# Scores of two heads on two halves of TensorE's rows, and the causal mask for the maxima split between VectorE and TensorE

## The chip, the cores and the metric

One core of a Trainium2 chip runs the whole program. The metric is the device time of one execution in microseconds, lower is better; the median of several runs is given. TensorE multiplies (weights are loaded beside it), VectorE, ScalarE and GpSimd compute element by element, SyncE issues transfers. Banks are the eight accumulation buffers that TensorE writes, 128 partitions of 512 fp32 each.

## What is computed

```python
x = x + 0.5 * ffn(layernorm(x))      # 8 experts, each token goes to the one with the largest gate
x = x + attn(layernorm(x))
x = x + 0.5 * ffn(layernorm(x))

def attn(x):                          # 8 sequences of 256 tokens, 128 wide, 16 heads of 8
    xn = x * rsqrt(mean(x * x) + 1e-6) * norm_w
    q, k, v = heads(xn @ Wq.T + bq), heads(xn @ Wk.T + bk), heads(xn @ Wv.T + bv)
    scores = where(causal, -inf, q @ k.T / sqrt(8))
    return xn + merge(softmax(scores) @ v) @ Wo.T + bo
```

## The kernel before

The program has three parts: a first expert layer, the attention, a second expert layer. Each expert layer first routes (gate logits, a chain of small VectorE operations in `route_pick`, `route_prob` and `route_slot`, then `dispatch` on GpSimd, which scatters 16 tiles of tokens with one indirect DMA each), then works through 23 tiles of tokens sorted by expert. The change touches only the attention and what runs beside it.

**Numbers and scores.** fp32 q and k are split into three bf16 parts, whose products are stacked along the partitions: 6 blocks of 8 rows are the 48 rows of one head (`JROWS`). `qz` holds q, `ks` holds k, two buffers of each for alternate sequences. Before, a pair of heads (j = 0 and 1) lies on 96 rows, and `qz` has zeros where the other head of the pair stands, so that one product over 96 rows gives one head's scores. Scores are computed twice. `scores_q` gives them with queries on the partitions, plus the causal mask, which TensorE adds as a product of the identity with a table; `max_unit` on VectorE takes each query's maximum from it. GpSimd splits the maxima into three bf16 parts (`max_split`), TensorE transposes them (`turn_max`), ScalarE copies them (`max_copy`), and SyncE's queue carries them as three more rows into `qz` (`max_rows`, 99 rows then). `scores_k` gives the scores with keys on the partitions and the maximum already subtracted; `exp_unit` on ScalarE takes exp into `pT`; `mask` on GpSimd sets what is above the diagonal to zero; `pv` on TensorE multiplies with v, four heads on four column groups of 32.

**Order.** A step is one sequence, in two halves of eight heads (four pairs); a half has six units, U0 to U5, each one bank of 512 columns. Step b computes `scores_k` of sequence b and, unit by unit beside it, `scores_q` of sequence b + 1. Before, U0, U1, U3 and U4 are early units, each one pair with keys 0 to 127 and all queries (for `scores_q` queries 128 to 255 and all keys); U2 and U5 are late units, two pairs with the other 128 keys (for `scores_q` queries and keys 0 to 127). `scores_q` uses banks 0 and 1, `scores_k` banks 2 and 3. Each engine's order is written out by hand; semaphores count units (`a_s` scores_q done, `a_mx` maxima, `a_st` scores_k done, `a_e` exps, `a_pm` masks, `a_pv` pv calls). `pv` of the half's first pairs (pp = 0) is issued behind U4 and waits for two masks, that of the others behind U1 of the next half and waits for all four. Between the units stand the products of the sequence before: `out_copy` on ScalarE, `turn_out` (transposes, one per 128 queries, banks 7 and 6), `normalise` on VectorE, `turn_norm`, a copy on ScalarE, `project`, `add_out` on VectorE. GpSimd also does the `residual` operations, 0.7 us each, between masks. Steps 1 to 4 stand in a loop of two iterations, the others are written out. SyncE's queue carries splits to DRAM (`split_stores`), loads them again as stacks (`stack_load`, four transfers per half) and `max_rows`, strictly one behind the other. `late_routing` places gate products of the second expert layer inside step 7, and `last_mask`, `late_stats` and the routing chain run on VectorE at its end; `ln_scale` on GpSimd stands between its masks and its scatters.

## Time and profile before

| | |
|---|---|
| median of 3 runs | 318.89 us (318.65 to 320.3) |
| profiled execution | 317.4 us, its span 315.3 us |
| TensorE busy | 271.4 us, 86% of the span, 2368 products |
| VectorE busy | 212.2 us, 67% |
| GpSimd busy | 185.7 us, 59% |
| ScalarE busy | 149.2 us, 47% |
| mean granted TensorE clock | 0.961 |

The span goes from the first to the last instruction of the profiled execution; the rest of its time lies around it. Busy shares are means over three parts with different limits: the attention steps lie between about 124 and 237 us of the span, the two expert layers on either side. Products overlap in TensorE and their ends are modelled, so start-to-start times are what a product costs in a row of them.

### The profile page before, as it was taken

The numbers are of one execution on the slowest core, as the hardware profiler recorded it, in microseconds if no ns is written. First come the engines' busy times: TensorE is split into PE (matmuls) and PEld (weight loads), VectorE is DVE, ScalarE is ACT, GpSimd is POOL, SyncE is SP. The second block draws the span as 40 slices with busy tenths as digits, with TensorE's granted clock in tenths as the row PEclk, the third lists the DMA queues.
The fourth block names the chain that finished last, engine by engine and source line by source line (L and its number), as shares of the span: only waits on it lengthen the run. The fifth ranks groups of instructions, "written<-read, shape, count | busy, mean of one in ns | idle before, by whom it ended". The sixth has DMA issues, their size and how long they took to land.

```text
span 315.3 us, 7921 instructions
## 1 busy us (share of the span) xinstructions
PE 271.4 (86%) x2368; PEld 219.5 (70%) x2368; DVE 212.2 (67%) x685; ACT 149.2 (47%) x362; POOL 185.7 (59%) x332
## 2 busy tenths in 40 slices
PE   7724999999997778999989999998977759999980
PEld 6724999999994544656656565665646658999970
DVE  4956058888539568986657777776587744888860
ACT  2300076666206613676656667666541007666620
POOL 7587815445726313786767787888647740555561
PEclk9999999999999996999999999999976799999997
DMA  6974232221041733552433522110001143122100
GB/s 184 397 313 122 60 80 55 68 67 32 17 133 41 202 109 112 165 166 87 135 95 115 157 74 70 58 55 2 5 10 45 56 113 91 49 68 67 30 21 0
DMA packets 34388, 29.37 MB, mean 93 GB/s; under 512 B 4109, under 2 KB 28818, under 8 KB 34353
## 3 DMA queue, kind: packets, MB, share of 16 engines
q1 hardware_dynamic: 29696, 23.52, 25.1%
q0 software_dynamic: 2496, 4.27, 4.3%
q10 hardware_dynamic: 2160, 1.14, 1.4%
q8 instruction: 18, 0.29, 0.4%
q14 instruction: 18, 0.14, 0.1%
HBM read 17.08 MB, written 12.55 MB: 94 GB/s over the span
## 4 chain that ended last, share of the span: by engine, by line
PE 48%; POOL 16%; issue 9%; DMA 9%; DVE 9%; SPq 4%; ACT 2%; POOLq 1%; ACTq 0%; DVEq 0%
PE bank L1291 12%; PE bank L1302 11%; POOL disp_d L479 7%; PE bank L1448 4%; PE bank L1420 3%; PE bank L1396 3%; POOL pT L574 2%; PE bank L1426 2%; DMA row<-in_x 2%; PE bank L1393 2%; SPq L406 2%; POOL row L470 2%; PE bank L1283 2%; PE bank L1401 2%; DMA disp_d<-row,slot 2%
## 5 line engine op out<-in xcount | busy, mean ns | idle before, releaser
L746 ACT ACTIVATE pT<-bank 128x512 f32<-128x512 f32 x96 | 56.5, 600 | 43.0 <-PE bank L1426 29.2
L1056 DVE TENSOR_REDUCE mh<-bank 128x2 f32<-128x512 f32 x64 | 42.1, 683 | 10.1 <-PE bank L1396 9.9
L1302 PE MATMUL bank<-experts,hT 128*128 x368 | 48.9, 276 | 0.0
L1291 PE MATMUL bank<-xsT,ew 128*128 128x128 f32 x368 | 48.8, 276 | 0.1
L1222 PE MATMUL bank<-zero 128*128 128x128 f32 x268 | 37.3, 305 | 10.5 <-DVE rowi L934 4.7
L574 POOL TENSOR_SCALAR_AFFINE_SELECT pT<-pT 128x512 f32<-128x512 f32 x62 | 40.2, 651 | 9.4 <-ACT pT L746 9.3
L1302 PEld LDWEIGHTS bank<-experts,hT 128*128 128x128 f32 x368 | 44.8, 192 | 0.5 <-issue 0.3
L1291 PEld LDWEIGHTS bank<-xsT,ew 128*128 128x128 f32 x368 | 44.7, 192 | 0.5 <-issue 0.2
L1222 PEld LDWEIGHTS bank<-zero 128*128 128x128 f32 x268 | 35.8, 219 | 11.0 <-DVE rowi L934 4.7
L664 ACT ACTIVATE hT<-bank,ew 128x128 f32<-128x128 f32 x92 | 28.9, 365 | 28.7 <-PE bank L1291 28.7
L941 DVE TENSOR_SCALAR hT<-bank,ew 128x128 f32<-128x128 f32 x92 | 28.0, 346 | 21.3 <-PE bank L1291 19.9
L479 POOL DMA_INDIRECT disp_d<-row,slot x32 | 32.3, 1009 | 13.3 <-issue 13.3
L487 POOL DMA_INDIRECT out<-ys_sb,xs_sb x23 | 22.6, 983 | 29.2 <-DVE ys_sb L965 27.7
L487 POOL DMA_INDIRECT x_d<-ys_sb,xs_sb x23 | 22.8, 991 | 24.1 <-DVE ys_sb L965 22.8
L652 ACT ACTIVATE xq<-xs_sb 128x128 f32<-128x128 f32 x46 | 22.5, 492 | 28.8 <-DMA xs_sb<-disp_d 28.8
L1060 DVE TENSOR_REDUCE mh<-bank 128x4 f32<-128x512 f32 x32 | 22.1, 690 | 19.3 <-PE bank L1405 19.3
L1420 PE MATMUL bank<-qz,ks 99*128 99x512 bf16 x64 | 24.8, 390 | 1.9 <-DMA qz<-mT 1.7
L1396 PE MATMUL bank<-ks,qz 96*128 96x256 bf16 x128 | 25.4, 281 | 0.0
L949 DVE TENSOR_SCALAR ew<-experts 128x644 f32 x46 | 22.4, 494 | 2.4 <-issue 1.8
L1448 PE MATMUL bank<-pT,va 128*32 128x256 f32 x256 | 20.9, 398 | 1.8 <-DVE pT L1182 1.5
L957 DVE TENSOR_TENSOR yb<-bank,ew 128x128 f32<-128x128 f32 x46 | 13.4, 292 | 12.8 <-PE bank L1302 10.0
L1393 PE MATMUL bank<-cb 128*128 128x256 bf16 x64 | 18.1, 283 | 1.6 <-DMA ks<-sp_d 1.3
(140 smaller groups left out, 465.9 us busy)
## 6 DMA issues: line engine op xcount, KB each, us to landing
sp_d<-spl SPq DMA_DIRECT2D x32, 192.0 KB, 2.5
experts<-in_experts SPq DMA_DIRECT2D x8, 578.0 KB, 9.5
qz<-sp_d SPq DMA_DIRECT2D x32, 96.0 KB
ks<-sp_d SPq DMA_DIRECT2D x32, 96.0 KB
xs_sb<-disp_d SPq DMA_DIRECT2D x46, 66.0 KB, 1.9
row<-in_x SPq DMA_DIRECT2D x4, 256.0 KB, 5.2
row<-x_d SPq DMA_DIRECT2D x4, 256.0 KB, 3.6
disp_d<-pad ACTq DMA_DIRECT2D x12, 66.0 KB
```

The source lines that it names most:

```text
L479: pool.indirect_dma_start(disp_d[f][:, :], bass.IndirectOffsetOnAxis(ap=slot[:, t:t + 1], axis=0), row[:, t, :], None).then_inc(d_tok[f], 16)
L487: pool.indirect_dma_start(target[:, :], bass.IndirectOffsetOnAxis(ap=xs_sb[:, t % RING, ID:ID + 1].bitcast(U32), axis=0), ys_sb[:, t % OUT ...
L574: pool.affine_select(out=p_, in_=p_, pattern=[[0, 4], [1, P]], compare_op=ALU.is_ge, fill=0.0, base=0, channel_multiplier=-1).then_inc(a_p ...
L664: mm = act.activation(hT[:, par, c, :], bank[2 + 2 * par][:, c * P:(c + 1) * P], ACT.Relu, bias=ew[:, k, HID + c:HID + c + 1])
L746: act.activation(pT[:, u, :], bank[2 + u % 2][:, :], ACT.Exp, scale=SCALE).then_inc(a_e, 1)
L1056: dve.tensor_reduce(mh[:, half, 1, :, 2 * pp + w], bank[u % 2][:, :].rearrange("p (h n) -> p h n", h=2), AX.X, ALU.max).then_inc(a_mx, 1)
L1222: pe.matmul(bank[b][:, 0:P], zero[:, :], zero[:, :], start=True, stop=True)
L1291: mm = pe.matmul(bank[2 + 2 * (k % 2) + c // 2][:, (c % 2) * P:(c % 2 + 1) * P], ew[:, k % WRING, c * P:(c + 1) * P], xsT[:, k % 2, :], st ...
L1302: mm = pe.matmul(bank[6 + k % 2][:, 0:D], hT[:, k % 2, c, :], w2.rearrange("p a c -> p (a c)"), start=(c == 0), stop=(c == HC - 1))
L1396: mm = pe.matmul(ov[:, j, :], qz[k][0:SROWS, half, j, pair - 4 * half, P:T], ks[k][0:SROWS, pair, :], start=False, stop=True, **MM_BANK)
L1420: mm = pe.matmul(ov, ks[k][0:KROWS, pair, 0:P], qz[k][0:KROWS, half, :, pair - 4 * half, :], start=True, stop=True, **MM_BANK)
L1448: mm = pe.matmul(o[32 * h:32 * h + 32, pp * T:(pp + 1) * T], va[:, k, 0, 8 * j + pair, :], pT[:, 3 * pp + h // 2, j * T:(j + 1) * T], star ...
```

## The change

- Heads of even and odd j no longer share rows with zeros: j = 0 lies on partitions 0 to 47 (and its three maxima rows on 48 to 50), j = 1 on 64 to 111 (and 112 to 114). The fill of `qz` goes. `max_rows` is two transfers.
- Units hold one j each: U0, U1 and U4, U5 are early (two pairs, one j), U2 and U3 late (all four pairs, one j). In a unit the `scores_k` product of a head of one j and the `scores_q` product of a head of the other j are issued in turn.
- `scores_q` has three banks (0, 1, 6). Its mask comes from TensorE in late units and for sequence 0; elsewhere `tensor_tensor_reduce` on VectorE adds `msk` and takes the maximum, 256 keys of one head at a time, writing the sum back to the bank.
- `turn_max`, both `turn_out`, `turn_norm` and `project` share bank 7, so they wait for each other. `project` and `add_out` move one half later, `turn_out` of the second query tile into the second half, `pv` of the first pairs behind U5 with three masks awaited.
- The loops over steps 1 to 4 are written out, and the `turn` instructions that stood before the masks in them go.

```diff
-SROWS = 2 * JROWS
-MROW = SROWS
-KROWS = MROW + 3
+KROWS = JROWS + 3
+JBASE = P // 2
...
+LOWEST = -3e38
+QB = (0, 1, 6)
...
+        def unit(u):
+
+            late = u in (2, 3)
+            return late, 0 if late else 2 * (u // 4), 4 if late else 2
...
-                    rows_j = slice(JROWS * j, JROWS * (j + 1))
-                    for t, buf in ((0, qz[k][rows_j, half, j, :, :]),
+                    rows_j = slice(JBASE * j, JBASE * j + JROWS)
+                    for t, buf in ((0, qz[k][rows_j, half, :, :]),
...
-                sp.dma_start(qz[k][MROW:MROW + 3, half, :, :, :].rearrange("s j i n -> s (j i n)"), mT[:, half, :]
-                             ).then_inc(a_m[half], 16)
+                for j in range(2):
+                    sp.dma_start(qz[k][JBASE * j + JROWS:JBASE * j + KROWS, half, :, :].rearrange("s i n -> s (i n)"),
+                                 mT[12 * j:12 * j + 12, half, :]).then_inc(a_m[half], 16)
...
-                pool.memset(qz[k][:, :, :, :, :].rearrange("p h j i n -> p (h j i n)").bitcast(F32), 0.0
-                            ).then_inc(static_s, 1)
...
+            def mask(b, half, n):
+
+                pool.wait_ge(a_e, 12 * b + 6 * half + (2, 3, 4, 6)[n])
                 need(pool, a_pm, 8 * b + 4 * half + n - 3)
-                if not isinstance(b, int):
-                    pool.tensor_tensor(turn[:, n:n + 1], zero[:, 0:1], zero[:, 0:1], ALU.add)
-                if late:
-                    p_ = pT[:, 3 * pp + 2, :].rearrange("p (h n) -> p h n", h=4)
+                if n in (1, 2):
+                    p_ = pT[:, n + 1, :].rearrange("p (h n) -> p h n", h=4)
                 else:
-                    p_ = pT[:, 3 * pp:3 * pp + 2, :].rearrange("p u (j n) -> p (u j) n", j=2)[:, :, 0:P]
+                    p_ = pT[:, n // 3 * 4:n // 3 * 4 + 2, :].rearrange("p u (i n) -> p (u i) n", i=2)[:, :, 0:P]
                 pool.affine_select(out=p_, in_=p_, pattern=[[0, 4], [1, P]], compare_op=ALU.is_ge, fill=0.0,
                                    base=0, channel_multiplier=-1).then_inc(a_pm, 1)
...
-            with pool.Fori(0, 2) as i:
-                for k in range(2):
-                    for half in range(2):
-                        step(2 * i + 1 + k, half)
-            for b in (5, 6, 7):
+            for b in range(1, B):
...
-                need(act, a_pv, 2 * (2 * b + half - 1) + 1 + u // 3
-                     if not isinstance(b, int) or 2 * b + half > 0 else 0)
+                need(act, a_pv, 2 * (2 * b + half - 1) + (1 if u < 2 else 2)
+                     if 2 * b + half > 0 else 0)
...
-                    if u == 3 and half == 1 and not first:
+                    if u == 4 and half == 1 and not first:
...
-                pp, w = divmod(u, 3)
+                late, p0, heads = unit(u)
                 if u == 0:
                     need(dve, a_mb, 2 * b + half - 1)
-                if w < 2:
-                    dve.tensor_reduce(mh[:, half, 1, :, 2 * pp + w],
-                                      bank[u % 2][:, :].rearrange("p (h n) -> p h n", h=2), AX.X, ALU.max
-                                      ).then_inc(a_mx, 1)
+                top = mh[:, half, 0 if late else 1, 1 - u % 2, p0:p0 + heads]
+                if b == 0 or late:
+                    i1 = dve.tensor_reduce(top, bank[QB[u % 3]][:, :].rearrange("p (h n) -> p h n", h=heads),
+                                           AX.X, ALU.max)
                 else:
-                    dve.tensor_reduce(mh[:, half, 0, :, 2 * pp:2 * pp + 2].rearrange("p j i -> p i j"),
-                                      bank[u % 2][:, :].rearrange("p (h n) -> p h n", h=4), AX.X, ALU.max
-                                      ).then_inc(a_mx, 1)
+                    n = 512 // heads
+                    for m in range(heads):
+                        sc = bank[QB[u % 3]][:, m * n:(m + 1) * n]
+                        i1 = dve.tensor_tensor_reduce(sc, sc, msk[:, T - n:T], 1.0, LOWEST, ALU.add, ALU.max,
+                                                      top[:, m:m + 1])
+                i1.then_inc(a_mx, 1)
...
-                o = bank[7 - qt][:, :].rearrange("p (g j c) -> p g j c", g=NPAIR, j=2)
+                o = bank[7][:, :].rearrange("p (g j c) -> p g j c", g=NPAIR, j=2)
...
+                    if b >= 2 and (half, u) == (0, 0):
+                        add_out(b - 2)
                     if not first:
-                        if half == 0 and u == 5:
+                        if half == 0 and u == 4:
                             normalise(b - 1, 0)
                         if half == 1 and u == 0:
                             normalise(b - 1, 1)
-                        if half == 1 and u == 5:
-                            add_out(b - 1)
...
+            dve.memset(msk[:, 0:P], 0.0).then_inc(msk_s, 1)
+            dve.tensor_copy(msk[:, P:T], cst[:, C_MS:C_MS + P]).then_inc(msk_s, 1)
             for u in range(6):
                 max_unit(0, 0, u)
+            quad_vbias(3)
+            dve.wait_ge(msk_s, 2)
...
+            add_out(5)
...
+                dve.wait_ge(a_e, 12 * (B - 1) + 6 + (2, 3, 4, 6)[n])
...
+            def head(k, half, p_, j, top):
+
+                return (qz[k][JBASE * j:JBASE * j + top, half, p_, :],
+                        ks[k][JBASE * j:JBASE * j + top, 4 * half + p_, :])
+
+            def scores_q_waits(b, half, u):
+
                 if u == 0:
...
+                    pe.wait_ge(a_stk[b % 2][half], 64 * (b // 2 + 1))
+                need(pe, a_mx, 12 * b + 6 * half + u - 2)
+
+            def scores_q_part(b, half, u, m, masked=False):
+
+                late, p0, heads = unit(u)
+                n = 512 // heads
+                q_, k_ = head(b % 2, half, p0 + m, 1 - u % 2, JROWS)
+                return pe.matmul(bank[QB[u % 3]][:, m * n:(m + 1) * n], q_[:, 0:P] if late else q_[:, P:T], k_[:, 0:n],
+                                 start=not masked, stop=True, **(MM_BANK if masked else {}))
+
+            def scores_k_part(k, half, u, m):
+
+                late, p0, heads = unit(u)
+                n = 512 // heads
+                q_, k_ = head(k, half, p0 + m, u % 2, KROWS)
+                return pe.matmul(bank[2 + u % 2][:, m * n:(m + 1) * n], k_[:, P:T] if late else k_[:, 0:P],
+                                 q_[:, T - n:T], start=True, stop=True)
+
+            def scores_q_mask(u):
+
+                heads = unit(u)[2]
+                pe.matmul(bank[QB[u % 3]][:, :].rearrange("p (h n) -> p h n", h=heads)[:, :, 512 // heads - P:],
+                          ident_b, maskS.unsqueeze(1).broadcast_to((P, heads, P)), start=True, stop=False, **MM_BANK)
+
+            def scores_first(half, u):
+
+                scores_q_waits(0, half, u)
+                scores_q_mask(u)
+                for m in range(unit(u)[2]):
+                    mm = scores_q_part(0, half, u, m, masked=True)
                 mm.then_inc(a_s, 1)
 
...
+            def scores(b, k, half, u, more):
+
                 if u == 0:
...
+                    pe.wait_ge(a_m[half], 32 * (b + 1))
                 need(pe, a_e, 12 * b + 6 * half + u - 1)
...
+                if more:
+                    scores_q_waits(b + 1, half, u)
+                    if unit(u)[0]:
+                        scores_q_mask(u)
+                for m in range(unit(u)[2]):
+                    mk = scores_k_part(k, half, u, m)
+                    if more:
+                        mq = scores_q_part(b + 1, half, u, m, masked=unit(u)[0])
+                mk.then_inc(a_st, 1)
+                if more:
+                    mq.then_inc(a_s, 1)
...
-                pe.wait_ge(a_pm, 8 * b + 4 * half + 2 * pp + 2)
+                pe.wait_ge(a_pm, 8 * b + 4 * half + pp + 3)
...
+            def step(b, half, more, first=False):
+
+                k = b % 2
                 for u in range(6):
...
+                    scores(b, k, half, u, more)
                     if u == 1 and half:
                         pv(b, k, 0, 1)
                     elif u == 1 and not first:
                         pv(b - 1, 1 - k, 1, 1)
...
+                    if (half, u) == (0, 0) and b >= 2:
+                        project(b - 2)
+                    if (half, u) == (0, 2):
+                        pe.wait_ge(a_mtc, 2 * b + 1)
+                        need(pe, a_x, b - 1)
+                        turn_max(b, 1)
+                    if (half, u) == (0, 3) and first:
                         pe.wait_ge(q_r, NU)
...
+                    if (half, u) == (0, 4) and not first:
+                        pe.wait_ge(a_mtc, 2 * b + 2)
+                        turn_out(b - 1, 0)
+                    if (half, u) == (0, 5) and first:
+                        pe.wait_ge(a_mtc, 2)
                         quad_v(4)
...
+                    if u == 5:
                         pv(b, k, half, 0)
...
+                    if (half, u) == (1, 0) and not first:
+                        pe.wait_ge(a_an, 2 * b - 1)
+                        turn_out(b - 1, 1)
+                    if (half, u) == (1, 2) and more:
+                        if first:
+                            pe.wait_ge(q_vc, NU)
+                        need(pe, a_an, 2 * b)
+                        pe.wait_ge(a_mtc, 2 * b + 2)
+                        turn_max(b + 1, 0)
+                    if (half, u) == (1, 4) and not first:
+                        if more:
+                            pe.wait_ge(a_mtc, 2 * b + 3)
+                        turn_norm(b - 1)
                     if not more:
                         late_routing(half, u)
...
+            for b in range(1, B):
                 for half in range(2):
...
+                    step(b, half, b < B - 1)
+            project(6)
...
+            pe.wait_ge(a_an, 2 * B - 1)
             turn_out(7, 1)
```

## Rows read from the trace of the kernel before

**Rows 1.** Busy time of each engine (and instructions), TensorE clock, DMA share, GB/s, one step.

```profile
164.90:178.30 13.40, 13.31 (x145) 8.50 (x143) 9.46 (x18) 8.68 (x17) 10.37 (x30) 1.00 0.41 120
```

**Rows 2.** Timeline of TensorE, step 4: start, us, engine, line, operation, [idle before].

```profile
177.69 0.71 PE L1478 MATMUL bank<-wt,anT 128*128 128x128 f32 x4
178.23 0.39 PE L1426 MATMUL bank<-qz,ks 99*128 99x256 bf16 x2
178.46 0.38 PE L1401 MATMUL bank<-cb 128*128 128x512 bf16 x1
178.68 0.39 PE L1405 MATMUL bank<-ks,qz 96*128 96x128 bf16 x4
178.90 0.38 PE L1420 MATMUL bank<-qz,ks 99*128 99x512 bf16 x1
...
185.72 0.38 PE L1420 MATMUL bank<-qz,ks 99*128 99x512 bf16 x1
...
186.60 0.38 PE L1396 MATMUL bank<-ks,qz 96*128 96x256 bf16 x2
186.91 0.64 PE L1448 MATMUL bank<-pT,va 128*32 128x256 f32 x8
...
187.70 0.39 PE L1426 MATMUL bank<-qz,ks 99*128 99x256 bf16 x2
```

**Rows 3.** Timeline of TensorE in step 7.

```profile
219.33 0.80 PE L1420 MATMUL bank<-qz,ks 99*128 99x512 bf16 x2
...
230.96 0.44 PE L1472 MATMUL bank<-ident_t,an 128*128 128x128 f32 x2 [0.64 <-DVE an L1100]
...
231.48 1.06 PE L1252 MATMUL bank<-wgc,gT 128*128 128x8 f32 x8
```

**Rows 4.** Timeline of GpSimd behind step 7.

```profile
238.06 0.19 POOL L468 TENSOR_SCALAR vs<-mv 128x2 f32<-128x2 f32 x1 [0.54 <-DVE mv L1169]
...
255.61 1.22 POOL L479 DMA_INDIRECT disp_d<-row,slot  x1 [0.30 <-issue]
```

**Rows 5.** Groups by line and shape: busy us, mean ns | idle before, releaser.

```profile
L1056 DVE TENSOR_REDUCE mh<-bank 128x2 f32<-128x512 f32 x64 | 42.1, 683 | 10.1 <-PE bank L1396 9.9
...
L1448 PE MATMUL bank<-pT,va 128*32 128x256 f32 x256 | 20.9, 398 | 1.8 <-DVE pT L1182 1.5 <-POOL pT L574 0.3
...
L569 POOL TENSOR_TENSOR turn<-zero 128x1 f32<-128x1 f32 x32 | 6.2, 195 | 11.5 <-ACT pT L746 11.5
...
L1107 DVE TENSOR_TENSOR row<-bank,row 128x256 f32<-128x256 f32 x4 | 1.7, 420 | 0.4 <-PE bank L1478 0.4
```

**Rows 6.** Timeline of ScalarE, steps 3 and 6.

```profile
178.66 0.60 ACT L746 ACTIVATE pT<-bank 128x512 f32<-128x512 f32 x1 [0.60 <-PE bank L1426]
...
208.79 0.36 ACT L753 COPY mT<-bank 24x256 bf16<-24x256 bf16 x1
209.11 0.60 ACT L746 ACTIVATE pT<-bank 128x512 f32<-128x512 f32 x1
209.61 0.58 ACT L759 COPY oT<-bank 128x512 f32<-128x512 f32 x1
```

**Rows 7.** Timeline of GpSimd, step 6.

```profile
211.52 0.64 POOL L574 TENSOR_SCALAR_AFFINE_SELECT pT<-pT 128x512 f32<-128x512 f32 x1
212.13 0.72 POOL L521 TENSOR_TENSOR res<-res,rows 128x256 f32<-128x256 f32 x1
212.81 0.64 POOL L574 TENSOR_SCALAR_AFFINE_SELECT pT<-pT 128x512 f32<-128x512 f32 x1
```

**Rows 8.** Timeline of SyncE's DMA queue, steps 3 and 4.

```profile
176.88 0.37 SPq L392 DMA_DIRECT2D sp_d<-spl  x1
...
181.30 0.70 SPq L406 DMA_DIRECT2D ks<-sp_d  x1
182.54 0.77 SPq L411 DMA_DIRECT2D qz<-mT  x1
```

**Rows 9.** Timeline of TensorE, step 2.

```profile
159.10 0.39 PE L1420 MATMUL bank<-qz,ks 99*128 99x512 bf16 x1 [1.69 <-DMA qz<-mT]
```

176 lines of the change are left out of this document (43 added, 133 removed).

## The prediction

> **What bounds the kernel now.** I read the page's first part (the table above), then the busy time of each engine step by step, then single engines' timelines inside a step. A step is one sequence (256 tokens) of the attention loop, two halves of eight heads with six units each: U0 to U5, a bank of scores per unit for `scores_k` and one for `scores_q`. TensorE is the busiest engine of the span, but that is a mean over stages. In a steady step the reader is to see TensorE busy 13.31 of 13.40 us, VectorE 9.46, ScalarE 8.68, GpSimd 10.37 [rows 1]: TensorE paces the steps. Step 4 starts at 178.90, its second half at 185.72 [rows 2], step 7 at 219.33 [rows 3]: steps 4 to 6 take 13.48 us each. Behind step 7 the bound changes: GpSimd waits 0.54 us for statistics of sequence 6 at 238.06 and then issues scatters one after another to 255.61, with 0.30 us of issue between [rows 4]. What comes late at 238.06 comes late at the end.
>
> **The change, part by part.** *Products.* An early unit (256 keys) had one `scores_k` product of 512 columns, a mask product of 256 and two `scores_q` products of 256. Columns are what costs: 512 take 0.22 us from start to start (178.46 to 178.68), four times 128 the same (178.68 to 178.90) [rows 2]. So a half streamed 8192 columns, 3.5 us. Now `scores_k` has 3072, `scores_q` 3072 and the mask 1024 (late units only). Heads of even j lie on partitions 0 to 50, of odd j from 64 on, and each k product is followed by a q product on the other half of the array's rows, into another bank. If a pair runs in the time of one, a half streams 4096 columns: 1.76 us, 1.7 less. The trace has no row tiles. Its nearest row is `pv` on four column groups: 256 products of 398 ns are busy 20.9 us together [rows 5], some five at a time. That bounds a pair between the time of one (0.11 us for 256 columns) and of two; I take one, since that row too is an array cut into parts.
>
> *Switches.* `pv` gives a price on the other side. The two score products before it start at 186.60 and have streamed by 186.82; `pv` starts at 186.91, 0.09 later [rows 2]. I take 0.10 us for each switch between whole and cut array; the lower bound is nothing, if 64-row products are no switch, the upper 0.2, twice the row. A half had four switches and gets eleven: around the transposes or projections behind U0 and U4, around the mask products of U2 and U3, around two `pv`. The Trainium skill (TensorEngine Tiling (Array Packing), Key Properties) says that a change of tiling mode drains the engine, and that tiles run independently. The trace agrees for the 128x32 tiles, 0.09 us; no run here shows 64-row tiles. By that rule all eleven are paid.
>
> *The chain inside a half* is then what counts, for TensorE's own sum is only 6.8 less 1.7 plus 0.7, 5.8 us. `pv` of the first pairs now stands behind U5 and needs three masks, not two, since both late units hold heads of all pairs. From U0: U0 0.22, four products of `project` 0.54 (177.69 to 178.23), U1 0.22, the `pv` of the half before 0.79 (186.91 to 187.70), U2's mask 0.22 [rows 2], then 0.49 to its exp (the last of four pairs starts 0.165 in, and the exp began 0.32 behind the second product that follows 178.23 [rows 2, 6]), and four switches: 2.88. From there the exp 0.60 [rows 6], on GpSimd a mask 0.61, a residual operation 0.68, the next mask 0.64 [rows 7], hand-overs twice 0.07 (ScalarE's start shows 0.04), then `pv` 0.79 and the next half's U0: 3.46. Together 6.34 us. In a first half ScalarE makes it longer: from U2's exp (2.88) 0.50 to `max_copy`, 0.32 to U3's exp, 0.50 to `out_copy`, its 0.58 [rows 6], 0.1, `turn_out` (0.54 as `project`), two switches, U5 0.22, `pv` 0.79: 6.6. A step is 12.95 us instead of 13.48. Score products lose 3.4 us a step; 0.5 arrive.
>
> *VectorE.* Eight reductions of 512 per step, 683 ns each, become sixteen `tensor_tensor_reduce` of 256 with a mask from SBUF. The trace has none. Nearest is the addition of 256 from a bank, 420 ns; the other end is 683 each, if the write-back and the read-out cost as much as half the elements [rows 5]. I take 420, the same two operands and elements: VectorE's step goes from 9.46 to 10.7, below 12.95, so it is hidden by the chain; at 683 it is 14.9. The Trainium skill (VectorE: DVE Perf Modes, Two Vector instructions with no wait between them) counts an operation that also reads out an accumulator as two instructions; no run here shows it, and it lies between these ends. The third bank lets TensorE run one unit further ahead of the maxima. TensorE idles 0.09 us a step [rows 1], so that gains nothing.
>
> *The maxima's rows.* `max_rows` becomes two transfers on SyncE's queue, 0.77 us of issue each. Queued behind the second are stores and loads, from 176.88 to 182.00 in a half with a store, and behind those the next `max_rows`, at 182.54 [rows 8]; U0 of the next half waits for its rows. The queue's round in such a step is 1.6 + 5.12 + landing + 3.74 from U0 to the end of `max_copy` (2.88 + 0.50 + 0.36). Landing took at most 3.18 (U0 at 185.72 didn't wait [rows 2, 8]) and at least its issue, 0.77; I take 2.5, between them and nearer to the upper, since loads go in front. That gives 13.0, as long as the chain; 3.18 gives 13.6. Once TensorE has waited 1.69 for these rows [rows 9]; I keep that wait. Step 0, with stores in both halves, gains nothing for that reason.
>
> *Hidden edits.* The `turn` instructions (6.2 us in all [rows 5]), the loops and the fill of `qz` go from GpSimd, which waits for exps and tiles there; without that cover a `turn` was 0.2 us. `msk` is built while VectorE waits for the first loads. `quad_vbias`(3) moved ahead of `quad_rest` costs up to 0.68 there, as a reduction of 512; the third bank saves TensorE about as much in the same place.
>
> *The end of the attention.* `project`(5) moves into step 7, and `pv` of its first half waits for the third mask, which stands behind `ln_scale` on GpSimd. The second gate's logits follow that `pv`, so `route_pick` and `normalise`(6,0) on VectorE are a `pv` late, 0.8 us. And `turn_out`(6,1) shares bank 7 now: TensorE waits for `normalise`(6,0) right behind U0 of the second half. Before, it waited at 230.96 for both, with U1, U2, `pv`, ranks and the third gate's transposes already issued, and that gate's logits followed at 231.48 [rows 3]. Now all of these come after the wait: `turn_out` 0.54, U1 0.22, `pv` 0.79, ranks and transposes (put at 0.54, as four products), 0.49 to U2's exp, 0.50, the gate's copy 0.58 as `out_copy`, switches 0.4: 4.06 us from `normalise`(6,0) to these logits. I put `normalise`(6,0) half a microsecond ahead of the old wait, so it was 1.0; 3.0 later. Then `pv`, whose mask now stands behind `route_pick`, and `project`(6) come before `add_out`(6), 1.33 us, less 0.3 for the last exp, which no longer ends last: 1.0. The sum, 4.8 us, meets the statistics awaited at 238.06. Bounds: 0 if the wait is covered, 6 if TensorE's clock falls in it.
>
> **Sum.** Steps 1 to 6: six by 0.5, 2.9 less. The end: 4.8 more. 315.3 and 2.1 around the span are 317.4 profiled; 319.3. The median shown, 318.89, lies 1.5 above its profile: 320.8, say 321.0.
>
> **Rivals.** (a) *Switches cost nothing*: 12 halves by 0.4, and 0.8 at the end, 5.6 less: 315.4, faster. For it: the array is cut by rows, not by columns as in `pv`. Against: the 0.09. It decides below 0.03 us a switch. (b) *The end is covered*: `normalise`(6,0) is done before TensorE needs it: 316.2, faster. Against it: TensorE did wait for it at 230.96. (c) *The pairs don't overlap*, so the change doesn't do what it says: U0, U1 and U2 0.22 longer each, 0.66 by 12 halves: 328.9. For it: no row here shows row tiles. (d) *SyncE's queue*: the wait of 1.69 in each of steps 1 to 4: 327.8. For it: the wait happened once. Against: 185.72 didn't wait. (e) *VectorE becomes the bound*, 14.9 a step: six by 1.95, 332.7. For it: two reads and a write on one bank.
>
> **Chances.** Forecast 0.48, with a range of its own of 318.5 to 323.5; (a) 0.15, (b) 0.10, (c) 0.12, (d) 0.10, (e) 0.05. A change within 0.5% (317.3 to 320.5) is about what a measurement can't tell from none. Faster takes (a), (b) and an edge of the forecast, 0.26; same the forecast's lower part, 0.21; slower the rest, 0.53. The range reaches from (a) to (c): 315 to 329.
>
> **What would show it.** Right: products on the two halves of the array that start almost together; gaps of 0.1 us at each switch; steps near 13 us with TensorE clearly idle, ended by GpSimd's mask in front of `pv`; sixteen reductions near 0.42 us; TensorE waiting some 3 us for `normalise` in step 7. Wrong: steps below 12.3; steps above 13.6 with VectorE full, or with the rows' transfer as releaser; score products one behind the other; scatters that start behind step 7 as early as now.

## The result: 334.6 us, and the profile after

| | before | after |
|---|---|---|
| median of 4 executions | 318.77 us | 334.63 us |
| profiled execution, its span | 317.4, 315.3 us | 333.28, 331.2 us |
| mean granted clock of TensorE | 0.961 | 0.924 |
| TensorE busy in the span | | 267.2 us (81%) |

The change makes the kernel slower, 1.0415 times (95% interval 1.0315 to 1.0515). Ratios, here and below, count undisturbed executions alone, medians count all. The forecast was 321.0, with a range to 329. The direction was right; of 15.9 us between the two profiled executions it had foreseen 1.9.

First the stretches of the profile after, cut at U0 of each step (step 0 to step 7, the last one cut at 240.09); the columns are the stretch, its length, busy time and instructions of TensorE, its weight loads, VectorE, ScalarE and GpSimd, the granted clock (1.00 is 2.4 GHz, 0.50 is 1.2 GHz), DMA share, GB/s.

```profile
124.29:140.11 15.82, 12.95 (x129) 6.29 (x130) 13.49 (x42) 8.70 (x16) 11.00 (x22) 0.68 0.57 168
140.11:153.66 13.55, 10.32 (x151) 5.22 (x148) 10.48 (x43) 8.47 (x17) 9.07 (x21) 1.00 0.36 105
153.66:170.42 16.76, 13.71 (x151) 6.50 (x152) 10.81 (x42) 8.52 (x17) 8.94 (x21) 0.80 0.34 97
170.42:184.41 13.99, 11.06 (x150) 5.62 (x151) 10.57 (x42) 8.65 (x18) 9.71 (x22) 1.00 0.40 117
184.41:198.54 14.13, 11.06 (x150) 5.65 (x150) 10.57 (x42) 8.58 (x17) 9.27 (x22) 1.00 0.37 110
198.54:214.18 15.64, 12.54 (x150) 6.08 (x150) 12.18 (x51) 8.58 (x17) 10.43 (x24) 0.89 0.17 54
214.18:228.20 14.02, 11.07 (x151) 5.64 (x151) 12.06 (x51) 8.59 (x17) 11.62 (x26) 1.00 0.10 33
228.20:240.09 11.89, 8.45 (x84) 5.65 (x85) 6.29 (x25) 5.04 (x10) 5.80 (x13) 1.00 0.01 2
240.09:260.30 20.21, 14.84 (x104) 8.99 (x105) 9.44 (x46) 5.63 (x13) 9.11 (x11) 0.58 0.07 21
```

The same of before, steps 0, 2 and 5 (step 2 holds the wait of [rows 9] at full clock):

```profile
123.58:137.05 13.47, 13.08 (x122) 8.01 (x121) 11.93 (x19) 8.95 (x16) 9.58 (x21) 0.88 0.61 176
...
150.46:165.54 15.08, 13.37 (x145) 8.44 (x143) 9.55 (x18) 8.71 (x18) 10.39 (x30) 1.00 0.41 115
...
192.28:205.53 13.25, 13.22 (x146) 8.37 (x144) 10.39 (x27) 8.81 (x18) 10.64 (x25) 1.00 0.21 62
```

Three things stand in these lines. TensorE's own work fell from 13.3 to 11.06 us a step, as it should. The steps didn't: those at full clock take 13.6 to 14.1 us, some 3 us of it TensorE's idle time. And steps 0, 2, 5 and the end have a clock below 1.00 and are the long ones. The kernel before has low clock too, in its step 0 (0.88) and behind step 7: over the 20.21 us that begin 11.89 us behind U0 of step 7, the last stretch above, it has 0.70 where the changed kernel has 0.58.

```profile
231.22:251.43 20.21, 15.53 (x104) 12.40 (x103) 14.94 (x81) 4.81 (x13) 14.52 (x17) 0.70 0.12 38
```

The losses: 0.7 us ahead of step 0 (124.29 for 123.58), 2.4 in step 0, 5.8 in steps 1 to 6, 7.0 behind U0 of step 7 (331.2 less 228.20, for 315.3 less 219.33).

Not all that step 2 loses is clock. Its second half waits 1.69 us for the rows of the maxima, at full clock, and so did step 2 of the kernel before. Behind that wait the clock falls: the second half takes 8.42 us, that of step 4 takes 6.45.

```profile
162.00 0.39 PE L1403 MATMUL bank<-qz,ks 51*128 51x256 bf16 x1 [1.69 <-DMA qz<-mT]
```

```profile
162.00:170.42 8.42, 8.09 (x75) 3.52 (x76) 5.21 (x20) 4.31 (x9) 3.28 (x8) 0.62 0.15 50
...
192.09:198.54 6.45, 5.44 (x74) 2.65 (x74) 4.98 (x20) 4.38 (x9) 4.22 (x11) 1.00 0.17 61
```

TensorE in step 4 after, for [rows 2]:

```profile
184.41 0.28 PE L1403 MATMUL bank<-qz,ks 51*128 51x256 bf16 x1 [0.22 <-DMA qz<-mT]
184.41 0.28 PE L1395 MATMUL bank<-ks,qz 48*128 48x256 bf16 x1
184.53 0.27 PE L1403 MATMUL bank<-qz,ks 51*128 51x256 bf16 x1
184.53 0.27 PE L1395 MATMUL bank<-ks,qz 48*128 48x256 bf16 x1
184.73 0.71 PE L1485 MATMUL bank<-wt,anT 128*128 128x128 f32 x4
...
189.32 0.63 PE L1472 MATMUL bank<-ident_t,oT 128*128 128x128 f32 x4 [1.03 <-ACT oT L756]
...
192.09 0.27 PE L1403 MATMUL bank<-qz,ks 51*128 51x256 bf16 x1 [1.03 <-DMA qz<-mT]
```

The two products of a pair start together, pairs 0.12 us apart; the second ends streaming at 184.64 and `project` starts at 184.73, a switch of 0.09. U0 of the second half then waits 1.03 us for the rows of the maxima. SyncE's queue says why, for [rows 8]:

```profile
181.57 1.56 SPq L419 DMA_DIRECT2D qz<-mT  x2
183.24 0.37 SPq L399 DMA_DIRECT2D sp_d<-spl  x1
...
188.01 0.70 SPq L413 DMA_DIRECT2D ks<-sp_d  x1
188.75 1.56 SPq L419 DMA_DIRECT2D qz<-mT  x2
```

`max_copy` had ended at 188.08, but from 181.57 on the queue worked off what stood ahead of these rows, with gaps of 0.4 us at most. The two transfers issue from 188.75; the second starts 0.8 later and has landed at 192.09, 3.34 behind the first one's start.

VectorE's new reductions, by line and shape over 138 to 228 us (count, busy us, mean ns; [rows 5]), and two of them in step 4:

```profile
L1056 DVE CUSTOM_DVE_ANT_0 bank<-bank,msk 128x256 f32<-128x256 f32 x100 | 40.0, 448 | 12.1 <-PE bank L1395 12.1
...
L1056 DVE DVE_READ_ACCUMULATOR2_ANT mh<- 128x1 f32 x100 | 14.1, 141 | 0.0
```

```profile
184.87 0.43 DVE L1056 CUSTOM_DVE_ANT_0 bank<-bank,msk 128x256 f32<-128x256 f32 x1 [1.04 <-PE bank L1395]
185.22 0.14 DVE L1056 DVE_READ_ACCUMULATOR2_ANT mh<- 128x1 f32 x1
185.22 0.47 DVE L1056 CUSTOM_DVE_ANT_0 bank<-bank,msk 128x256 f32<-128x256 f32 x1
```

Two instructions each, as the Trainium skill (VectorE: DVE Perf Modes, Two Vector instructions with no wait between them) counts it; but the read-out runs beside the next reduction, which starts 0.35 us behind the one before (184.87 and 185.22).

GpSimd in step 6, where `ln_scale` (L473, L475) stands between the masks, and TensorE's `pv` behind it:

```profile
217.68 0.64 POOL L575 TENSOR_SCALAR_AFFINE_SELECT pT<-pT 128x512 f32<-128x512 f32 x1 [0.80 <-ACT pT L743]
218.28 0.76 POOL L524 TENSOR_TENSOR res<-xn,rows 128x256 f32<-128x256 f32 x1
219.12 0.19 POOL L473 TENSOR_SCALAR vs<-mv 128x4 f32<-128x4 f32 x1
219.40 1.02 POOL L475 TENSOR_TENSOR row<-vs,mhalf 128x4 f32<-128x4 f32 x1
220.39 0.64 POOL L575 TENSOR_SCALAR_AFFINE_SELECT pT<-pT 128x512 f32<-128x512 f32 x1
```

```profile
221.08 0.64 PE L1455 MATMUL bank<-pT,va 128*32 128x256 f32 x8 [1.04 <-POOL pT L575]
...
240.09 1.12 PE L1472 MATMUL bank<-ident_t,oT 128*128 128x128 f32 x4 [2.86 <-DVE an L1096]
...
245.46 1.06 PE L1248 MATMUL bank<-wgc,gT 128*128 128x8 f32 x8 [1.15 <-ACT gT L629]
...
250.97 1.20 PE L1485 MATMUL bank<-wt,anT 128*128 128x128 f32 x4
```

The last three lines answer to [rows 3]: the wait for `normalise`, the third gate's logits (17.3 us behind U0 of step 7, before 12.15) and `project`(6).

### The profile page after: what moved, and what is told of

Its sections match the earlier page's. It is cut to its first block, busy times and chain, and to the rows that moved or that the text cites. A ratio compares the mean times of both kernels' runs of the same rounds, so it can differ in the third digit from the quotient of the medians.

```text
span 331.2 us, 7965 instructions
## 1 busy us (share of the span) xinstructions
PE 267.2 (81%) x2440; PEld 203.2 (61%) x2440; DVE 220.7 (67%) x855; ACT 148.1 (45%) x362; POOL 177.8 (54%) x298
## 4 chain that ended last, share of the span: by engine, by line
PE 44%; DMA 14%; POOL 10%; DVE 10%; SPq 9%; issue 8%; ACT 2%; POOLq 0%; DVEq 0%; ACTq 0%
PE bank L1287 11%; PE bank L1298 11%; DMA qz<-mT 7%; POOL disp_d L484 5%; PE bank L1403 5%; SPq L413 4%; PE bank L1455 4%; SPq L419 3%; PE bank L1472 2%; DMA row<-in_x 2%; PE bank L1485 2%; PE bank L1279 2%; PE bank L1450 2%; PE bank L1409 1%; DMA disp_d<-row,slot 1%
## 5 line engine op out<-in xcount | busy, mean ns | idle before, releaser
L743 ACT ACTIVATE pT<-bank 128x512 f32<-128x512 f32 x96 | 57.3, 603 | 57.2 <-PE bank L1403 56.9
L575 POOL TENSOR_SCALAR_AFFINE_SELECT pT<-pT 128x512 f32<-128x512 f32 x62 | 41.2, 666 | 37.3 <-ACT pT L743 37.3
L1056 DVE CUSTOM_DVE_ANT_0 bank<-bank,msk 128x256 f32<-128x256 f32 x112 | 44.8, 448 | 14.1 <-PE bank L1395 14.1
L1403 PE MATMUL bank<-qz,ks 51*128 51x256 bf16 (+1 forms) x256 | 37.9, 264 | 6.9 <-DMA qz<-mT 5.6
L1395 PE MATMUL bank<-ks,qz 48*128 48x256 bf16 (+1 forms) x256 | 37.8, 263 | 0.0
L484 POOL DMA_INDIRECT disp_d<-row,slot x32 | 31.5, 984 | 11.7 <-issue 11.4
L1050 DVE TENSOR_REDUCE mh<-bank 128x4 f32<-128x512 f32 (+1 forms) x40 | 26.8, 686 | 11.4 <-PE bank L1395 11.3
L1455 PE MATMUL bank<-pT,va 128*32 128x256 f32 x256 | 23.1, 437 | 10.8 <-POOL pT L575 8.1
L1403 PEld LDWEIGHTS bank<-qz,ks 51*128 51x128 bf16 x256 | 15.2, 98 | 25.0 <-issue 10.3
L950 DVE TENSOR_TENSOR yb<-bank,ew 128x128 f32<-128x128 f32 x46 | 13.4, 292 | 13.1 <-PE bank L1298 10.3
```

The lines of the kernel that those rows point to most:

```text
L484: pool.indirect_dma_start(disp_d[f][:, :], bass.IndirectOffsetOnAxis(ap=slot[:, t:t + 1], axis=0), row[:, t, :], None).then_inc(d_tok[f], 16)
L575: pool.affine_select(out=p_, in_=p_, pattern=[[0, 4], [1, P]], compare_op=ALU.is_ge, fill=0.0, base=0, channel_multiplier=-1).then_inc(a_p ...
L743: act.activation(pT[:, u, :], bank[2 + u % 2][:, :], ACT.Exp, scale=SCALE).then_inc(a_e, 1)
L1056: i1 = dve.tensor_tensor_reduce(sc, sc, msk[:, T - n:T], 1.0, LOWEST, ALU.add, ALU.max, top[:, m:m + 1])
L1395: return pe.matmul(bank[QB[u % 3]][:, m * n:(m + 1) * n], q_[:, 0:P] if late else q_[:, P:T], k_[:, 0:n], start=not masked, stop=True, **( ...
L1403: return pe.matmul(bank[2 + u % 2][:, m * n:(m + 1) * n], k_[:, P:T] if late else k_[:, 0:P], q_[:, T - n:T], start=True, stop=True)
```

## The experiments

Four theories. *Queue*: the rows of the maxima bind steps 1 to 4. *GpSimd*: what stands between the masks binds. *End*: the order on VectorE, as predicted. *Clock*: TensorE now idles, its clock falls, and that costs what the order doesn't explain. Times are medians, ratios are to the kernel before on the same chip. Where no line is quoted, steps are cut at U0 from the run's profile as above, and each profile is of one execution. Edits are in short form; comments say where a line stands.

**Loads on ScalarE's queue** (`loads_on_scalar`)

```diff
+ if u == 5 and half == 1 and b + 2 < B:          # ScalarE, behind U5's exp
+     act.wait_ge(q_std[b + 2], 64)
+     stack_rows(act, b + 2, b % 2, 1, (1,))      # odd heads' two loads
...
+ stack_rows(sp, b, k, half, range(1 if b >= 2 and half == 1 else 2))   # SyncE issues the others
```

> The changed kernel, with the two loads of odd heads for each second half issued on ScalarE's queue behind U5's exp (some 0.45 us each there, where ScalarE waits 1.6 for TensorE) instead of on SyncE's; SyncE's queue has 1.5 us less in front of the next rows of the maxima. Theory of the queue: these rows bind steps 1 to 4, 14.1 us around (U0 to the rows' issue 3.7, issue and queue 7.2, the rows of the other half 3.3). Without the 1.5 the rows of the second half go out as soon as max_copy has ended, 0.67 earlier; the wait at U0 of the second half falls from 1.0 to about 0.35 us, steps 1, 3 and 4 take 13.4 instead of 14.0, and the time falls by 2 to 3 us, by up to 5 if the wait of 1.7 in step 2, after which TensorE's clock was at 1.2 GHz, goes too. Rival, GpSimd's masks bind the steps: the wait moves to pv behind the third mask, steps stay at 14.0, and the time is within 0.5 us.

332.92 us, 1.0465 (1.0399 to 1.053). Steps 2 to 4 of its profile:

```profile
158.03:171.46 13.43, 11.07 (x150) 5.63 (x150) 10.56 (x42) 8.59 (x17) 9.49 (x22) 1.00 0.40 121
171.46:184.52 13.06, 11.06 (x150) 5.64 (x150) 10.57 (x42) 8.59 (x17) 9.11 (x22) 1.00 0.41 124
184.52:197.83 13.31, 11.07 (x150) 5.63 (x150) 10.57 (x42) 8.58 (x17) 9.44 (x22) 1.00 0.41 122
```

The steps did what the theory says, and U0 of the second half waits at most 0.2 us for the rows. The time didn't: steps 2 to 6 are 6.5 us shorter than in the changed kernel's profile (3.6 of it the clock, which held in steps 2 and 5), but step 0 began 2.7 us later, steps 0 and 1 took 16.90 and 14.12 at a clock of 0.60 and 0.85, and the end, with its order unchanged, was 2.2 us longer. Steps 5 and 6 stayed at 14.2 and 14.0, `pv` waiting 1.05 for GpSimd.

**normalise(6,0) ahead of route_pick(1,0)** (`normalise_first`)

```diff
- route_pick(1, 0); normalise(6, 0); normalise(6, 1)
+ normalise(6, 0); route_pick(1, 0); normalise(6, 1)
```

> The changed kernel with one exchange on VectorE in step 7: normalise(6,0) ahead of route_pick(1,0). Theory of the end as predicted: TensorE's wait for normalise(6,0) of 2.86 us in front of turn_out(6,1) goes, the third gate's logits and add_out(6) come some 3 us earlier, and the whole is 2.5 to 3.5 us faster. Rival, the end is set by TensorE's clock at 1.2 GHz between 240 and 260 us and not by the order: the wait goes, but what it had covered is waited for at the ranks (which need route_pick), and less than 1 us comes back.

328.63 us, 1.0323 (1.0256 to 1.039), for 1.0415: some 3 us less by the ratios, as expected, though the intervals overlap. From U0 of step 7 (227.15) to the span's end it is 99.95 us, for 103.0, and `turn_out` has no wait:

```profile
236.13 1.01 PE L1472 MATMUL bank<-ident_t,oT 128*128 128x128 f32 x4
```

So the step of the forecast holds: 3.0 us of the end.

**Products in the waits** (`products_in_waits`)

```diff
+ idle_work(2, 6 if half else 2)    # ahead of U0's wait for the rows; b > 0
+ idle_work(4 + half, 4)            # ahead of pv's wait for the masks
+ idle_work(7, 6)                   # ahead of turn_out
```

> The changed kernel with TensorE kept busy in its waits: products of 128 columns of zeros (0.14 us each) in front of U0 (6 in second halves, 2 in first), in front of pv of the half's first pairs (4) and of turn_out (6), from step 1 on. Nothing else is changed; where a wait is shorter than these products they cost up to 0.5 us a half. Theory of the clock: steps 2 and 5 took 16.8 and 15.6 us instead of 14.0 because the granted clock had fallen to half after such waits, and the end of the attention likewise; the clock stays at 1.0 from 140 to 236 us, these steps come to 14 to 14.5, and the time falls by 3 to 6 us. Rival, a low clock only stretches products that have slack: the clock stays up and the time stays within 1 us or grows by what the products cost, up to 5 us.

348.01 us, 1.0911 (1.0822 to 1.1001). Each of steps 2 to 5 was alike, for instance:

```profile
177.01:193.67 16.66, 16.56 (x195) 10.89 (x194) 10.57 (x42) 8.59 (x17) 9.33 (x22) 1.00 0.34 97
```

The clock stayed up, so far as the theory says; the products took 0.25 us each, not 0.14, and made TensorE full. The edit was too large to price the clock.

**The kernel before with its rows in two transfers** (`before_rows_in_two`)

```diff
- sp.dma_start(qz[k][MROW:MROW + 3, half, :, :, :].rearrange("s j i n -> s (j i n)"), mT[:, half, :]
-              ).then_inc(a_m[half], 16)
+ for s0, s1 in ((0, 1), (1, 3)):
+     sp.dma_start(qz[k][MROW + s0:MROW + s1, half, :, :, :].rearrange("s j i n -> s (j i n)"),
+                  mT[8 * s0:8 * s1, half, :]).then_inc(a_m[half], 16)
...
- pe.wait_ge(a_m[half], 16 * (b + 1))
+ pe.wait_ge(a_m[half], 32 * (b + 1))             # both have to land; so too where ScalarE waits
```

> The kernel before with one part of the change alone: the rows of the maxima go as two transfers (row 1, then rows 2 and 3), one behind the other on SyncE's queue. Theory of the queue: the second transfer starts 0.8 us later and lands 2.5 us behind its start, so the queue's round goes from about 12.5 to 14.0 us, past the 13.4 of a step; steps 1 to 4 take 0.3 to 0.7 longer, the time 1.5 to 4 us more. Rival, the rows were hidden and stay hidden: within 0.5 us.

319.19 us, 1.0014 (0.998 to 1.0048): the rival's result. By itself the doubled transfer costs nothing measurable. The slack it uses up is small, though: in the one profile, of an execution of 321.63 us, TensorE waited six times for the rows in steps 0 to 4, 0.24 to 1.59 us, where the kernel before waited once. That it binds in the changed kernel because the round there is longer in its other parts too is argued, not tried.

**Both products of a pair on one row half** (`one_row_half`)

```diff
- q_, k_ = head(b % 2, half, p0 + m, 1 - u % 2, JROWS)
+ q_, k_ = head(b % 2, half, p0 + m, u % 2, JROWS)
```

and the same exchange where VectorE stores the maxima.

> The changed kernel with one part undone: the scores_q product of each pair is that of the head on the same half of the array's rows as its scores_k product, so that the two of a pair run one behind the other; columns, switches, order and results stay. Theory of the chain: products off the chain of a half have slack (TensorE is idle 2.4 to 3.0 us of 14.0 in a step), and only U0, U1 and U2 lie on it, 0.66 us a half; in steps 1 to 4 the rows' transfers bind and the loop through them holds U0, U1 and U2 as well. Steps go from 14.0 to about 15.3, the time up by 7 to 10 us. Rival, the side-by-side products are worth nothing where they lie: within 1 us. A second rival, TensorE becomes full: 12 half steps by 1.32, 14 to 16 us more.

391.2 us (381.65 to 392.71), far outside every number expected. One of its steps:

```profile
189.08:212.71 23.63, 22.89 (x152) 11.55 (x150) 11.73 (x42) 8.68 (x17) 9.30 (x22) 0.50 0.24 68
```

The clock was at 1.2 GHz from 158 to 270 us although TensorE was busy 22.9 of 23.6 us. This doesn't price the overlap, but it moved the study to the clock.

**Masks by TensorE again** (`masks_by_tensor`)

```diff
- if b == 0 or late:                              # VectorE: plain maximum
+ if True:
- if unit(u)[0]: scores_q_mask(u)                 # TensorE: mask product
+ scores_q_mask(u)
```

> The changed kernel with another part undone: the masks of the early units come by a product of 256 columns on TensorE, as in the late units and in the first sequence, and VectorE takes plain maxima (8 of 683 ns instead of 16 of 448 and 141 ns in a step: 9.4 us become 5.5). TensorE pays 0.11 us and two switches of 0.1 for each of four early units in a half. Theory of the chain, VectorE's longer maxima are hidden: three of the four lie on the chain of a half, 0.9 us a half less what the rows' wait covers, so steps of 15 to 16 us and 6 to 12 us more. Rival, VectorE's maxima bind the steps or delay the rows of the maxima: steps get shorter, 13 to 13.5 us, and 3 to 6 us come back.

338.17 us, 1.0604 (1.0528 to 1.0681) for 1.0415: some 6 us more, the least that was expected, and steps 3 and 4 took 13.8 and 14.3, not 15 to 16. VectorE's maxima don't bind. That these steps grew so little because the rows bind anyway is argued; U0 still waits 0.2 to 0.5 us for them.

**Four moves** (`four_moves`)

```diff
+ the edits of loads_on_scalar and normalise_first
- RES_AT = [(0, 1), (0, 3), (1, 1)]
+ RES_AT = [(0, 0), (0, 3), (1, 0)]               # residual operations off the mask chain
- if b >= 5 and (half, n) == (0, 1): ln_scale(2, b - 5)
+ if b >= 5 and (half, n) == (0, 3): ln_scale(2, b - 5)
+ if b == B - 1 and half: project(6)              # ahead of pv(7, 1, 0)
```

> The changed kernel with four moves of order: the loads on ScalarE's queue and normalise(6,0) first, as in the two runs before; on GpSimd the residual operations and ln_scale stand behind the first or the last mask of a half instead of between the masks; and project(6) stands ahead of the last but one pv, which waits for VectorE's mask. Theory of the chain: with the queue and GpSimd out of the way steps 2 to 6 take 12.9 to 13.1 us (13.25 before the masks were moved, 14.1 in steps 5 and 6), normalise gives 3 us and project(6) 1 to 2 us; about 322 to 325. If TensorE's clock sets the steps instead, they stay uneven (13 to 16 us), and the time is above 327.

333.87 us, 1.0542 (1.0464 to 1.0621). Steps 2 to 4 came to 13.1 to 13.3, but one of the moves was wrong: VectorE's `ln_bias` waited 2.2 us for `ln_scale`, and behind it `normalise` and TensorE's transposes of the maxima,

```profile
207.48 0.27 PE L1471 MATMUL bank<-cb,mb 128*24 128x128 bf16 x2 [1.49 <-DVE an L1103]
```

behind which the clock fell; steps 5 and 6 took 14.6 and 16.6.

**The moves mended** (`moves_mended`), the four moves but for one:

```diff
- if b >= 5 and (half, n) == (0, 3): ln_scale(2, b - 5)
+ if b >= 5 and (half, n) == (0, 1): ln_scale(2, b - 5)
```

> The four moves without the one that failed: ln_scale stands behind the second mask again, since VectorE's ln_bias waited 2.2 us for it and with it normalise and the transposes of the maxima (1.5 us of TensorE in steps 5 and 6). Theory of the chain: steps 2 to 4 at 13.1 to 13.3, 5 and 6 at 14.1, the end 4 us shorter than the changed kernel's: 323 to 327. Theory of the clock: with more idle time of TensorE there are more falls, steps of 15 to 16.5 us among them, and it is not below 328.

325.85 us, 1.0192 (1.0123 to 1.0261); one of its four executions, of 795 us, stands alone and unexplained, and the median of the other three is 324.41. Steps 2 to 6: 13.4, 13.1, 13.3, 13.9, 14.0, all at 1.00. Step 0 took 15.3 at 0.68.

**Zeros at the start** (`zeros_at_start`)

```diff
+ def zero_work(b, n):
+     for _ in range(n):
+         pe.matmul(bank[b][:, 0:P], zero[:, 0:P // 2].bitcast(BF16), zero[:, 0:P // 2].bitcast(BF16),
+                   start=True, stop=True)
+ zero_work(7, 14)                                # ahead of turn_max(0, 0)
+ if u == 3: pe.wait_ge(q_r, 4); zero_work(5, 10) # ahead of scores_first(1, 3)
```

> The changed kernel with 24 products of 128 bf16 columns of zeros (0.055 us each) in two waits of TensorE ahead of step 0: 14 in front of the first transposes of the maxima, which waited 1.03 us for GpSimd, and 10 in front of the fourth unit's mask, which waited 0.70 for VectorE. Theory of the clock: the granted clock was 0.5 from 124 to 134 us in the changed kernel's trace, behind these waits, and step 0 took 15.8 us for 13.5 before; if TensorE is busy in them the clock stays at 1.0 or is back sooner, step 0 takes 13.5 to 14.5 and the time falls by 1.5 to 4 us. Rival, the clock falls all the same, since it fell in the kernel before at the same place: within 1 us.

335.27 us, 1.0485 (1.041 to 1.0561): the rival's result. The clock held past both waits and fell later instead, at 130 us behind waits of 0.79 and 0.47, and at 140 behind one of 1.72.

**Waits filled** (`waits_filled`), the edits of `zeros_at_start` and

```diff
+ if b == 0 and u == 5: zero_work(5, 6)           # step 0; also 4, 10 and 22 elsewhere in it
+ if b > 0: zero_work(2, 12 if half else 2)       # ahead of U0's wait for the rows
+ zero_work(5, 8)                                 # ahead of pv in second halves
+ if b in (5, 6): zero_work(4, 12)                # and in first halves
+ zero_work(7, 12 if b < 7 else 0)                # ahead of turn_out
```

> The changed kernel with TensorE kept busy in the waits of the attention by short products of zeros (128 bf16 columns, 0.055 us each, so that a wait of 1.03 us takes 12 and a step's fill is 1.9 us, less than it idles; the earlier fill cost 0.25 us a product, 5.5 us a step): ahead of step 0 as in the run with zeros at the start, in step 0 in front of U2, of the transposes of the maxima, of U5 and of the second half's pv, then in each step in front of turn_out (12), of U0 (12 and 2) and of pv (8; 12 in the first halves of steps 5 and 6). The end is not filled. Theory of the clock: the granted clock stays at 1.0 from 112 to 236 us, step 0 takes 14 us (15.8), steps 2 and 5 take 14 (16.8 and 15.6), and the time falls by 5 to 7 us to 327 to 330. Rival, a low clock stretches only what has slack: within 1.5 us.

333.88 us, 1.0506 (1.0435 to 1.0576). Steps 0 and 2:

```profile
124.09:138.56 14.47, 12.60 (x178) 7.54 (x179) 13.38 (x43) 8.68 (x16) 11.44 (x23) 1.00 0.66 187
...
151.59:167.20 15.61, 13.42 (x186) 7.54 (x186) 10.58 (x42) 8.58 (x17) 9.71 (x23) 1.00 0.40 113
```

The clock was 1.00 from 110 to 230 us, as expected, and step 0 lost 1.3 of the 2.4 us that it had above the kernel before. But the products weren't free: step 2 took 15.6, and steps 3 to 6 took 13.8 to 15.0 instead of 14.0 to 15.6. From U0 of step 0 to U0 of step 7 it is 101.7 us for 103.9; the end, which wasn't filled, took 105.5 for 103.0, and the sum came out even.

**Moves and fill** (`moves_and_fill`), both, with fewer products where waits are shorter, and in the end:

```diff
+ zero_work(6, 14)                                # ahead of logits(1, 2) and of pv(7, 1, 0)
+ zero_work(6, 12)                                # ahead of pv(7, 1, 1)
+ zero_work(6, 10)                                # ahead of turn_out(7, 0)
```

> The mended moves with the waits filled by the same short products, fewer where the moves shortened the wait (U0 2 and 6, second halves' pv 4), and in the end of the attention as well (in front of the third gate's logits, of the last two pv and of turn_out). If chain and clock together are what the change costs: step 0 13.5 to 14.5, steps 1 to 4 at 13.1 to 13.3, 5 and 6 at 14.1, the clock at 1.0 throughout, the end 4 to 6 us shorter than the changed kernel's: 316 to 321, at or below the kernel before. If something else costs time, above 324.

322.62 us, 1.0145 (1.0087 to 1.0203), between the two ranges expected. Step 4, and with it all from step 0 to step 6, was at full clock, and from U0 of step 7 (225.36) to the end it took 95.9 us, what the kernel before took (96.0).

```profile
183.28:196.71 13.43, 12.84 (x174) 6.97 (x174) 10.58 (x42) 8.58 (x17) 9.32 (x22) 1.00 0.41 122
```

Steps 2 to 6 sum to 68.7 us, before to 68.9. What is left of its profile's 6 us lies ahead of step 2: U0 of step 0 at 128.65, for 123.58 before, with the clock at 0.5 from 116 to 124 us.

**Transposes of the maxima earlier** (`turn_early`), on the mended moves:

```diff
- if (half, u) == (0, 2): turn_max(b, 1)          # TensorE; so too (1, 2) to (1, 1)
+ if (half, u) == (0, 1): turn_max(b, 1)
- if u == 2: max_copy                             # ScalarE
+ if u == 1: max_copy
```

> The mended moves with one more: the transposes of the maxima behind U1 instead of U2, and max_copy behind U1's exp, so that the rows leave some 1.0 us earlier. Theory of the chain: what is left above 12.95 a step is the way of the rows (3.7 us from U0 to the end of max_copy, 3.3 to the landing, 7.0 a half); it becomes 6.0, TensorE's waits for the rows of 0.2 to 0.6 us in each half go, steps 2 to 4 take 12.6 to 13.0, and the time is 1 to 2.5 us below the mended moves' 325.9. Rival, GpSimd's masks or turn_out bind next: steps stay at 13.1 to 13.4 and the time is within 1 us of 325.9.

329.57 us, 1.0362 (1.0259 to 1.0465): a miss. Steps 2 to 5 took 13.3 to 13.7. The wait moved to GpSimd's split of the maxima:

```profile
180.06 0.27 PE L1471 MATMUL bank<-cb,mb 128*24 128x128 bf16 x2 [0.74 <-POOL mb L569]
```

**The same, filled** (`turn_early_filled`), as in `moves_and_fill` but for a few products ahead of U0 and `pv`, and

```diff
- idle_work(0, 10)                                # ahead of the first scores
+ idle_work(0, 15)
```

> turn_early with the waits filled as in the run with moves and fill, and five more of the products of zeros (0.25 us each) that stand ahead of the first scores, where TensorE waits 1.3 us for the first loads and the clock fell at 114 us in most runs. If chain and clock are all: clock at 1.0 from 100 to 230 us, step 0 from 124 us, steps of 12.7 to 13.2, 316 to 319, about the kernel before. If something else costs time: above 320.

324.14 us, 1.016 (1.0088 to 1.0232); clock 1.00 from 110 to 230 us, steps 2 to 4 at 13.5. The end, with the same fill as there, took 100.4 us, not 95.9; its clock was 0.50 from 230 to 234 all the same. No better than moves and fill, and not below the kernel before.

**Fill on half of the rows** (`half_row_fill`)

```diff
- zero[:, 0:P // 2].bitcast(BF16), zero[:, 0:P // 2].bitcast(BF16)
+ zero[0:P // 2, 0:P // 2].bitcast(BF16), zero[0:P // 2, 0:P // 2].bitcast(BF16)
```

> The run with filled waits again, with products of zeros that use 64 of the array's 128 rows instead of all; their columns, count and places are the same. Theory of the rows: what holds the clock up is how much of the array works, so these fill products hold it less well; the granted clock falls to 0.5 for stretches of the attention again, as in the changed kernel (mean below 0.95 from 130 to 230 us), and the time is 2 to 5 us above the full-row fill's 333.9. Rival, only idle time counts: the clock stays at 1.0 from 130 to 230 us and the time is within 1.5 us of 333.9.

335.74 us, 1.0476 (1.0353 to 1.0599): the median is 1.9 above that of `waits_filled`, the ratio lower (1.0476 for 1.0506). Undecided: the clock was 0.50 from 126 to 134 us, where the full rows' fill held it, and 1.00 from 142 on.

**One row half, filled** (`one_row_half_filled`), on `waits_filled`:

```diff
- q_, k_ = head(b % 2, half, p0 + m, 1 - u % 2, JROWS)
+ q_, k_ = head(b % 2, half, p0 + m, u % 2, JROWS)
```

> The run with both products of a pair on the same half of the array's rows, its waits filled by products of zeros on all rows as in the run with filled waits. Theory that idle time alone makes the clock fall: with the fill it stays at 1.0, steps take 15.5 to 16.5 us (14.9 with side-by-side products and the same fill, 0.66 a half more on the chain) and the time is 338 to 346. Rival, products on half of the rows hold the clock down even when TensorE is never idle: 0.5 for most of the attention again, steps of 20 us and more, above 375.

343.99 us, 1.0801 (1.0732 to 1.087), below the same kernel without the fill by 47 in the median, by 39 in the fastest execution (342.45 for 381.65):

```profile
180.74:196.38 15.64, 15.51 (x186) 9.58 (x184) 10.75 (x42) 8.58 (x17) 9.27 (x21) 1.00 0.36 102
```

From 150 us on the clock was 1.00; from 118 to 142 it was 0.50, although TensorE was busy throughout. With the clock up the overlap's worth shows: steps 2 to 6 took 15.6 to 16.5 us against 13.8 to 15.6 in `waits_filled`, and the whole 1.0801 against 1.0506, some 9 us.

**Zeros in the kernel before** (`zeros_in_before`, `zeros_in_before_again`)

```diff
+ zero_work(6, 18)                                # ahead of turn_max(0, 0)
+ if u == 2: pe.wait_ge(q_r, 4); zero_work(5, 16)
```

> The kernel before with one thing added: products of zeros (128 bf16 columns, all rows) in the two waits of TensorE ahead of step 0, 18 in front of the first transposes of the maxima (1.24 us of wait) and 16 in front of the third unit's mask (1.11). Its granted clock was 0.5 from 119 to 127 us, behind these waits. Theory of the clock: it stays at 1.0 there, the first products of step 0 take half as long, and step 1 starts 1 to 2.5 us earlier; the time falls by 1 to 2.5 us. Rival, what is stretched there has slack against the loads and the maxima: within 0.7 us.

> The kernel before with 34 short products of zeros in two waits ahead of step 0, once more. If they gain what the first run showed, 0.985 to 0.992 of the kernel before; if that was chance, 0.995 to 1.002.

315.45 us, 0.9877 (0.98 to 0.9954), and again 315.83, 0.9945 (0.9915 to 0.9974). The stretch ahead of step 0, first in the filled kernel, then before:

```profile
118.00:127.00 9.00, 8.00 (x77) 4.94 (x75) 8.78 (x15) 4.37 (x7) 3.40 (x14) 1.00 0.28 88
```

```profile
118.00:127.00 9.00, 7.27 (x37) 3.99 (x37) 7.40 (x13) 3.30 (x6) 3.14 (x11) 0.62 0.42 122
```

This is the one form below both kernels, by half a per cent (the second ratio lies between the two ranges expected of it); it holds nothing of the change. By the span, step 1 began only 0.3 us earlier. But in that execution the first scores fell 1.73 us later; first the filled kernel, then before:

```profile
113.54 0.28 PE L1399 MATMUL bank<-cb 128*128 128x256 bf16 x1 [1.25 <-DMA ks<-sp_d]
...
136.74 0.39 PE L1426 MATMUL bank<-qz,ks 99*128 99x512 bf16 x1
```

```profile
111.81 0.28 PE L1393 MATMUL bank<-cb 128*128 128x256 bf16 x1 [1.32 <-DMA ks<-sp_d]
...
137.05 0.39 PE L1420 MATMUL bank<-qz,ks 99*128 99x512 bf16 x1
```

From the first scores to step 1 it is 23.20 us, and 23.22 in the second run's profile, for 25.24 before: 2.0 less, within the 1 to 2.5 expected. Though it rests on one profile of the kernel before, it is the plainest price of a low clock among these runs.

## Why the forecast was too low

*Side by side, and the switches: right.* Pairs start together, switches cost 0.09 to 0.10 us, and rivals (a) and (c) are out; so is (b), since TensorE did wait in step 7. The Trainium skill (TensorEngine Tiling (Array Packing), Key Properties) lets tiles run independently and drains at a change of mode; the trace now agrees with both, for 64-row tiles too.

*The chain inside a half: right.* `turn_out` of step 4 starts 4.91 us behind U0, 4.88 by the forecast's terms; the second half takes 6.45 for 6.34. With the queue cleared a step takes 13.1 to 13.4, forecast 12.95.

*VectorE: right.* Its step is busy 10.57 us, forecast 10.7; (e) is out.

*The maxima's rows: mis-sized, and rival (d) in part.* The round was put at 13.0. Its landing of 2.5 was good for the second transfer, but counts from its own start, 0.8 behind the first one's, and stores and loads took 5.5 (183.24 to 188.71), not 5.12. Measured, the round is 188.75 less 174.66, the same transfers one step earlier: 14.09, and steps 3 and 4, at full clock, follow it. `loads_on_scalar` shows it. Steps above 13.6 with the rows' transfer as releaser were among the forecast's own signs of being wrong.

*`ln_scale` between the masks: left out* for steps 5 and 6, though the forecast counted it in step 7. It and the residual operation hold `pv` back by 1.04 us in the first half; at full clock these steps take 14.0, not 12.95, and stay at 13.9 and 14.0 when the queue is cleared (`moves_mended`). No run took this wait out without putting another in its place, so its price is read from the trace.

*The end: direction and cause right, 4.8 forecast, 7.0 measured.* TensorE waited 2.86 us for `normalise`(6,0), forecast some 3, and the exchange on VectorE gave 3.0 back: from U0 of step 7 the profiles with the old order take 102.0 to 106.0 us (`one_row_half` aside), those with the exchange 99.7 to 100.8, but for `four_moves` (102.9) and `moves_and_fill` (95.9). What was missed goes with the clock: 0.58 from 240 to 260 us, 0.70 in the same stretch before. With the mended moves the end takes 99.7 us, and with fill in its waits 95.9 where the clock held, 100.4 where it fell all the same. The forecast had the clock only in a bound of 6.

*The sum's arithmetic.* Six steps by 13.48 less 12.95 are 3.2 us less, not 2.9, and (d) counts the wait of step 2 a second time. Neither changes the outcome.

*The step that failed* is the sum's silence on the clock of the attention itself, and with it the length of a step. The forecast foresaw "TensorE clearly idle" and priced idle time at nothing. By the profiles it missed 14.0 of the 15.9 us. Of these, 5.1 are steps that are too long at full clock: 3.0 in steps 1 to 4, whose round was put at 13.0 and measured 14.09, and 2.1 in steps 5 and 6, for `ln_scale`. Some 7 lie in stretches of low clock: 2.0 in the second half of step 2 (8.42 for 6.45), 1.6 in step 5 (15.6, where step 6 with the same waits took 14.0), 1.3 in step 0 (15.8, and 14.5 with its waits filled), and the 2.2 by which the end is above its 4.8. The last is put down to the clock without a run of the changed kernel that shows it. The rest, 1.8, lies in the start and in step 0.

That products in a wait hold the clock there is shown by five runs, though not everywhere (116 to 124 us in `moves_and_fill`, 230 to 234 in `turn_early_filled`). That the time follows is shown in the kernel before (2.0 us ahead of step 1) and where the fall was total (391 to 344 us). In the changed kernel it stays open how much a clock held for nothing would return: the products in `waits_filled` took back part of what they gave, 2.2 us net from step 0 to step 7, and between `moves_mended` and `moves_and_fill` lie 1.5 us by the ratios, within their intervals.

## What to carry to other kernels

Work taken off the engine that paces a kernel arrives only as far as the next chain allows, here none of 2.2 us a step, and at most 0.3 with the queue cleared; find that chain, with every instruction that a queue or an engine puts into it, before counting columns. Two transfers in place of one put the first one's issue in front of the second one's landing, on every turn of a loop that waits for both; where the loop has slack that costs nothing measurable, where it has none the loop gets longer. And on TensorE idle time is not free: look at the granted clock behind each wait, and where a wait can't go, a few short products in it may pay, in the old kernel as in the new.

## What the runs showed of the hardware

- Products on 48 to 51 rows, one behind the other, left TensorE at 1.2 GHz for over 100 us while it was busy 97% of the time (22.89 of 23.63 us in a step); with products on all rows in its waits the same kernel ran at 2.4 GHz from 150 us on. The Trainium skill (TensorE: Matmul & The Clock Gate, Part 1) ties the level to how busy TensorE has been; by the profile's count TensorE was busy here and the level was the lower one. Whether rows or gaps decide was not settled.
- Waits of 1 to 1.7 us were followed by a fall in some executions and steps and not in others: in the changed kernel those of step 5 were (203.46 and 205.45, then 1.2 GHz from 206 to 209), the same ones of step 6 were not.
- Two masks on GpSimd, 0.63 us each elsewhere, took 2.21 us from 137.64 on, while VectorE ran an operation of 1024 elements into bf16 beside them (137.20 to 138.77).
